# One transpose per tile of probabilities, and a router whose high and low weights share one stationary block

## The chip, the core and the metric

The kernel runs on one core of a Trainium2 chip. The core has TensorE (PE; its weight loads are a row of their own, PEld), VectorE (DVE), ScalarE (ACT), GpSimd (POOL) and SyncE (SP), which starts most of the transfers. The metric is the device time of one execution in microseconds, lower is better. Where a text speaks of the kernel before, its time is the median of three runs, 304.88 us (304.15 to 305.09).

## What is computed

One gated cross-attention block and one mixture-of-experts block, on 32 sequences of 64 tokens with 256 features. Cut to what matters:

```python
# x: (32, 64, 256), ctx: (32, 64, 256)
h = layernorm(x)
q, k_new, v_new = h @ wq.T, h @ wk.T, h @ wv.T
k = concat([ctx, k_new], axis=1)          # 128 keys per sequence: 64 of ctx, 64 new
v = concat([ctx, v_new], axis=1)
attn = softmax(q @ k.T / 16)              # no mask is applied
x = x + tanh(g_xattn) * (attn @ v) @ wo.T

h = layernorm(x)
probs = softmax(h @ gate_w.T)             # 8 experts, the two best of a token are kept
y = sum over the two of probs[e] * expert_e(h)       # silu(h @ fc1.T) * (h @ fc2.T) @ proj.T
y = y + sigmoid(h @ shared_gate_w.T) * shared(h)     # the same form, 704 wide
x = x + tanh(g_ffn) * y
```

All is float32. The kernel does its large products in split form: a value is kept as a high part, rounded to the type fp32r, and a low part, value minus high part, and a product is the sum of three matmuls, high by high, high by low and low by high (`THREE`).

## The kernel before, in words

The 2048 tokens are four chunks of 512 (`c`), each four tiles of 128 tokens (`j`). A tile holds two sequences (64 tokens each). The program is written out by hand for each engine, and the order in which each does its work is the order of the code; semaphores tie the engines together. It has these stages, in microseconds of the profiled execution: start (0 to 27), attention (27 to about 116), shared expert for three chunks together with loading of the expert weights (116 to 200), the 39 tiles of the routed experts (200 to 274), and the rest with the final sums.

In the attention stage a tile of scores is one bank of 128 rows (queries of both sequences) by 256 columns: the first half are new keys of both sequences, the second half keys of the context of both. A query needs the columns of its own sequence alone, so of each row two blocks of 64 are used. The work of one tile:

- `scores` (PE), six matmuls of 256 columns; `row_max` (VectorE), two reductions, one for each half of the partitions; `exps` (ScalarE), two exponentials, which write the used blocks into a buffer `PR` (one of two). The unused blocks of `PR` were set to zero at the start (L1233).
- `probs_t` (PE, L498): two transposes of 128x128, one for the new keys and one for the context.
- `probs_hi` (ScalarE) copies the 128x256 result to the high part `PT[0]`; `probs_lo` (VectorE) subtracts it to give the low part `PT[1]`. In the profile both stand under the helper's line and the names `ew_hi` and `ew_lo`, since the buffers are views of one large tensor (`EW`) that later holds the expert weights: L769 ACT `ew_hi<-bank` 128x256 and L1002 DVE `ew_lo<-bank,ew_hi` 128x256, 16 each, are these and nothing else.
- `values` (PE), twelve matmuls, then `v_hi` (ScalarE) and `v_lo` (VectorE), 128x512.
- `attend` (PE), six matmuls. The first waits for `probs_hi`, the second for `v_lo`, the third for `probs_lo`. `residual` (VectorE) adds the input and takes statistics.

Between these stand `project` for the next chunk, whose results `project_hi` (ScalarE) and `project_lo` (VectorE) split, and, for the chunk before, `second_norm`, `router` and `logits`. `router(c)` (PE) is six matmuls with 72 columns of weights as the stationary side (9 are used) and 512 tokens moving, three for each half of the features. Its output of 9 rows is copied by ScalarE, transposed by four small PE transposes (L539), and copied by VectorE (L1089) for the softmax of the router (L1117 on). ScalarE's `route_exp` is a part of that softmax. GpSimd makes the low parts of the context keys (L1468), the reciprocal roots of the norms, and issues the scatters; its first work waits for the constants.

In the code printed below, `own_keys` picks the columns of one sequence out of a bank, and `ring(base, j)` gives the count that frees one of two buffers.

## Time and profile before

| what | value |
|---|---|
| median of 3 runs | 304.88 us (304.15 to 305.09) |
| the profiled execution | 305.98 us, span 304.2 us |
| mean granted TensorE clock | 0.986 |
| PE busy | 276.9 us, 91% of the span, 1785 matmuls |
| DVE busy | 215.7 us, 71%, 698 instructions |
| ACT busy | 170.6 us, 56%, 399 instructions |
| POOL busy | 131.1 us, 43%, 163 instructions |
| DMA | 40.18 MB, mean 132 GB/s |

The span goes from the first to the last instruction; the execution's own time has 1.8 us more around it. Busy time is no critical path: an engine may be busy with work that nobody waits for. A matmul's duration in the rows overlaps the next one's, so what a matmul costs is read from the distance between starts, not from its length. The same holds, less strongly, for VectorE and ScalarE.

### The profile page before, as it was taken

Reading aid. Unit: us, or ns where it says so; the run is one execution under the profiler, and the core shown is the slowest. Engines: PE = TensorE matmul, PEld = TensorE weight load, DVE = VectorE, ACT = ScalarE, POOL = GpSimd, SP = SyncE. Lnnn points to the kernel's source line nnn. Section 1 sums busy time; section 2 is a strip of 40 time slices with the busy share of each in tenths; the row PEclk is TensorE's granted clock in tenths of the full one; section 3 lists DMA queues with packets and bytes.
Section 4 is the critical chain, followed back from the end, with each engine's and each line's share of the span. In section 5 each row is a group of like instructions: output and inputs, shape, how many; then the busy total and the mean of one; then the engine's idle time right before and its main releaser. Section 6 shows DMA issues by size and latency. Waiting matters only on the chain.

```text
span 304.2 us, 5865 instructions
## 1 busy us (share of the span) xinstructions
PE 276.9 (91%) x1785; PEld 249.0 (82%) x1785; DVE 215.7 (71%) x698; ACT 170.6 (56%) x399; POOL 131.1 (43%) x163
## 2 busy tenths in 40 slices
PE   0978989999999789799999999799999999999992
PEld 1867968888788667489888888689999999998891
DVE  2664777879968948766776775877787777863285
ACT  1565676777756546555325455456667666664230
POOL 1350361361587154732333000037777777786000
PEclk9997999999999999999999999999999999999996
DMA  6451107203028031433233665258888888866796
GB/s 196 173 176 69 70 11 239 82 21 122 1 77 280 1 110 53 151 130 120 92 123 128 188 232 185 59 134 139 136 136 138 137 137 143 126 71 69 239 353 239
DMA packets 30510, 40.18 MB, mean 132 GB/s; under 512 B 2960, under 2 KB 26640, under 8 KB 30480
## 3 DMA queue, kind: packets, MB, share of 16 engines
q1 hardware_dynamic: 22336, 29.53, 31.0%
q0 software_dynamic: 7152, 9.57, 19.0%
q10 hardware_dynamic: 992, 0.71, 0.9%
q8 instruction: 15, 0.25, 0.3%
q14 instruction: 15, 0.12, 0.1%
HBM read 22.68 MB, written 17.11 MB: 131 GB/s over the span
## 4 chain that ended last, share of the span: by engine, by line
PE 55%; DVE 23%; ACT 8%; issue 6%; POOL 3%; DMA 3%; DVEq 0%; ACTq 0%; SPq 0%; POOLq 0%
PE bank L415 43%; PE bank L654 6%; DVE ew_lo L1002 4%; ACT ew_hi L769 3%; PE bank L747 3%; DVE work L1332 3%; PE bank L703 3%; DVE xt_lo L1002 2%; ACT sh_hi L769 2%; DMA consts_sb<-consts_dram 2%; DVE work L1354 2%; DVE neg_max L1046 2%; ACT work L801 1%; DVE sh_lo L1002 1%; DMA weight_stage<-ew_dram 1%
## 5 line engine op out<-in xcount | busy, mean ns | idle before, releaser
L1522 POOL DMA_INDIRECT y_d<-work,dest_of_slot x39 | 60.5, 1552 | 56.3 <-DVE dest_of_slot L1378 54.7
L415 PE MATMUL bank<-ew_hi,xt_hi 128*128 (+2 forms) x172 | 53.8, 322 | 1.1 <-DVE xt_lo L1002 0.8
L415 PE MATMUL bank<-ew_lo,xt_hi 128*128 (+2 forms) x172 | 51.9, 302 | 0.0
L415 PE MATMUL bank<-ew_hi,xt_lo 128*128 (+1 forms) x133 | 40.5, 305 | 0.0
L1002 DVE TENSOR_TENSOR xt_lo<-bank,xt_hi 128x256 fp32r<-128x256 f32 (+2 forms) x90 | 35.7, 398 | 3.0 <-ACT xt_hi L769 1.5
L1482 POOL DMA_INDIRECT xs_d<-xn_all,slot_of_pair x32 | 32.0, 1001 | 10.1 <-issue 7.3
L415 PE MATMUL bank<-ew_hi 128*128 128x256 f32 (+1 forms) x100 | 31.5, 321 | 3.9 <-DVE ew_lo L1002 2.0
L1002 DVE TENSOR_TENSOR ew_lo<-bank,ew_hi 128x512 fp32r<-128x512 f32 (+1 forms) x41 | 22.7, 581 | 16.9 <-ACT ew_hi L769 16.8
L769 ACT ACTIVATE xt_hi<-bank 128x256 fp32r<-128x256 f32 (+1 forms) x90 | 32.7, 409 | 3.5 <-PE bank L747 2.2
L415 PE MATMUL bank<-xt_hi,sw_hi 128*128 128x512 f32 x88 | 34.6, 394 | 0.0
L415 PE MATMUL bank<-xt_lo,sw_hi 128*128 128x512 f32 x88 | 34.5, 392 | 0.0
L415 PE MATMUL bank<-xt_hi,sw_lo 128*128 128x512 f32 x88 | 34.4, 390 | 0.0
L415 PEld LDWEIGHTS bank<-ew_hi,xt_hi 128*128 128x128 f32 (+1 forms) x172 | 32.5, 189 | 1.7 <-DVE xt_lo L1002 1.0
L415 PEld LDWEIGHTS bank<-ew_lo,xt_hi 128*128 128x128 f32 (+1 forms) x172 | 32.7, 190 | 0.1
L415 PE MATMUL bank<-ew_hi,ew_lo 128*128 128x256 f32 (+1 forms) x100 | 31.1, 318 | 1.5 <-DVE ew_lo L1002 1.5
L415 PE MATMUL bank<-ew_lo,ew_hi 128*128 128x256 f32 (+1 forms) x100 | 30.8, 315 | 1.7 <-DVE ew_lo L1002 1.1
L769 ACT ACTIVATE sh_hi<-work 128x512 fp32r<-128x512 f32 (+1 forms) x24 | 15.2, 632 | 25.5 <-DVE work L1332 24.2
L654 PE MATMUL bank<-sw_hi,sh_hi 128*128 128x256 f32 x96 | 27.4, 290 | 2.0 <-DVE sh_hi L1002 1.9
L769 ACT ACTIVATE ew_hi<-bank 128x512 fp32r<-128x512 f32 (+1 forms) x45 | 21.7, 517 | 10.7 <-PE bank L415 6.9
L654 PE MATMUL bank<-sw_lo,sh_hi 128*128 128x256 f32 x96 | 27.0, 286 | 0.0
L930 ACT ACTIVATE work<-bank 128x512 f32<-128x512 f32 (+1 forms) x24 | 14.3, 594 | 21.9 <-PE bank L415 21.9
L415 PEld LDWEIGHTS bank<-ew_hi 128*128 128x128 f32 x100 | 19.5, 196 | 7.0 <-ACT ew_hi L769 3.7
(159 smaller groups left out, 688.5 us busy)
## 6 DMA issues: line engine op xcount, KB each, us to landing
work<-xs_d SPq DMA_DIRECT2D x39, 136.0 KB, 2.5
weight_stage<-ew_dram SPq DMA_DIRECT2D x10, 486.5 KB, 3.7
ew_hi<-y_d SPq DMA_DIRECT2D x8, 512.0 KB, 7.4
y_d<-work SPq DMA_DIRECT2D x6, 512.0 KB, 3.9
work<-ctx_t_dram SPq DMA_DIRECT2D x4, 512.0 KB, 3.5
xn_all<-x_dram SPq DMA_DIRECT2D x3, 512.0 KB, 6.5
xs_d<-pad_row SPq DMA_DIRECT2D x9, 136.0 KB, 1.8
weight_stage<-sw_dram SPq DMA_DIRECT2D x3, 384.0 KB, 3.2
```

Source lines behind the costliest of these rows:

```text
L415: last = nc.tensor.matmul(dst, a, b, start=(n == 0), stop=(n == len(pairs) - 1))
L654: last = nc.tensor.matmul(B[4 + t][:, 0:D], h[:, t * P:(t + 1) * P], w, start=(j == 0 and n == 0), stop=(j == S_FULL and n == len(parts) - 1))
L703: last = nc.tensor.transpose(rows_bank(n)[:, k * P:(k + 1) * P], EX[:, w, k * P:(k + 1) * P], ident)
L747: last = nc.tensor.transpose(B[4 + v][:, i * P:(i + 1) * P], EH[:, v, i * P:(i + 1) * P], ident)
L769: return nc.scalar.activation(dst, src, ACT.Copy, scale=scale)
L930: nc.scalar.activation(STH[0:rows, j % 2, :], B[pair(s, j)][0:rows, :], ACT.Silu).then_inc(a_th, 1)
L1002: return nc.vector.tensor_tensor(dst, src, hi.bitcast(F32), ALU.subtract)
L1046: last = nc.vector.tensor_reduce(nmx[r, j % 2:j % 2 + 1], own_keys(B[4 + j % 2], b), mybir.AxisListType.XY, ALU.max, negate=True)
L1332: nc.vector.tensor_tensor(SHF[0:rows, j % 2, :], STH[0:rows, j % 2, :], h2, ALU.mult).then_inc(v_h, 1)
L1354: nc.vector.tensor_scalar(SX2[:, t, :], B[4 + t][:, 0:D], GS[:, T:T + 1], None, ALU.mult).then_inc(v_z, 1)
L1482: nc.gpsimd.indirect_dma_start(out=xs_d, out_offset=bass.IndirectOffsetOnAxis(ap=POS[:, i, n:n + 1], axis=0), in_=XN[:, n, :], in_offset=N ...
L1522: nc.gpsimd.indirect_dma_start(out=y2_d, out_offset=bass.IndirectOffsetOnAxis(ap=IX[:, n:n + 1], axis=0), in_=EY[:, n % 4, :], in_offset=None,
```

## The change

The score columns get another order: new keys of sequence 0 (64), context keys of both (128, with the two sequences swapped), new keys of sequence 1 (64). The exponentials of a query now go into one dense block of 128 columns (`PR` is half as wide and needs no zeros). One transpose turns this block. In the result, the four quarters of 64x64 belong to two different sequences and two different kinds of key; `probs_hi` and `probs_lo` put each quarter where it belongs in `PT`, two quarters with one instruction on partitions 0 to 63 and two with one on 64 to 127. The other four quarters of `PT` must be zero: GpSimd clears them once, at the start, in place of VectorE's clearing of `PR`. The helper `own_probs` gives the destination; `own_half` does the same for the new keys, whose blocks are now apart.

In the router, the 72 stationary columns hold the high parts in columns 0 to 8 and the low parts in columns 32 to 40. A matmul with the high part of the tokens gives both products at once. So four matmuls do for six; the product of low weights and low tokens comes along and is added too. ScalarE copies 41 rows for 9, the transposes have 41 columns for 9, and VectorE adds the two parts where it copied.

The names in the profile change with it: line numbers move by a few (L415 is L419, L498 is L501, L1002 is L1007).

```diff
+RW_LO = 32
+RW_ROWS = RW_LO + N_E + 1
-NEW, OLD = 0, 1
+OLD = slice(SEQ, 3 * SEQ)
...
-        RW = [sb(f"router_{s}", [P, KD, RW_COLS], F32R) for s in ("hi", "lo")]
+        RW = sb("router", [P, KD, RW_COLS], F32R)
-        KC = [[e.rearrange("p (m j x n) -> p m j x n", m=KD, j=TPC, x=2) for e in half]
+        KC = [[e.rearrange("p (m j n) -> p m j n", m=KD, j=TPC) for e in half]
-        PT = [e[:, 8704:9216].rearrange("p (r x n) -> p r x n", r=2, x=2) for e in EW]
+        PT = [e[:, 8704:9216].rearrange("p (r x s n) -> p r x s n", r=2, s=2, x=2) for e in EW]
...
-        LGT = WK[0:N_E + 1, 4096:4608]
-        PR = WK[:, 4608:5120].rearrange("p (r x s n) -> p r x s n", r=2, x=2, s=2)
+        LGT = WK[0:RW_ROWS, 4096:4608]
+        PR = WK[:, 4608:4864].rearrange("p (r x n) -> p r x n", r=2, x=2)
+        ZERO = WK[:, 4864:5120]
...
             def scores(c, j):
-                             [(q[a][:, m, j * P:(j + 1) * P], keys[b][:, m, j, :, :].rearrange("p x n -> p (x n)"))
+                             [(q[a][:, m, j * P:(j + 1) * P], keys[b][:, m, j, :])
...
             def probs_t(c, j):
-                for x in range(2):
-                    last = nc.tensor.transpose(B[j % 2][:, x * P:(x + 1) * P],
-                                               PR[:, j % 2, x, :, :].rearrange("p s n -> p (s n)"), ident)
-                last.then_inc(p_pt, 1)
+                nc.tensor.transpose(B[j % 2][:, 0:P], PR[:, j % 2, :, :].rearrange("p x n -> p (x n)"), ident).then_inc(p_pt, 1)
...
             def attend(c, j):
-                             [(PT[a][:, j % 2, x, :], VO[b][:, j, x, :]) for x in range(2) for a, b in THREE], waits)
+                             [(PT[a][:, j % 2, x, :, :].rearrange("p s n -> p (s n)"), VO[b][:, j, x, :]) for x in range(2) for a, b in THREE], waits)
...
             def router(c):
-                             [(RW[a][:, k, :], XT[b][:, c, k, :]) for k in range(KD) for a, b in THREE], waits)
+                             [(RW[:, k, :], XT[b][:, c, k, :]) for k in range(KD) for b in range(2)], waits)
...
             def logits(c):
-                    last = nc.tensor.transpose(B[7][:, j * 16:j * 16 + N_E + 1], LGT[:, j * P:(j + 1) * P],
-                                               ident[0:N_E + 1, 0:N_E + 1])
+                    last = nc.tensor.transpose(B[7][:, j * 2 * RW_LO:j * 2 * RW_LO + RW_ROWS], LGT[:, j * P:(j + 1) * P],
+                                               ident[0:RW_ROWS, 0:RW_ROWS])
...
             def project_hi(c, i):
-                    copy(KC[c % 2][0][:, i - 2, :, NEW, :], bank[:].rearrange("p (j n) -> p j n", j=TPC)).then_inc(a_qk, 1)
+                    copy(own_half(KC[c % 2][0], i - 2), bank[:].rearrange("p (j s n) -> p j s n", j=TPC, s=2)).then_inc(a_qk, 1)
...
             def exps(c, j):
-                    last = nc.scalar.activation(PR[r, j % 2, :, b, :], own_keys(B[4 + j % 2], b),
+                    last = nc.scalar.activation(PR[r, j % 2, :, :], own_keys(B[4 + j % 2], b),
...
             def probs_hi(c, j):
-                copy(PT[0][:, j % 2, :, :], B[j % 2][:, 0:2 * P].rearrange("p (x n) -> p x n", x=2)).then_inc(a_pt, 1)
+                if (c, j) == (0, 0):
+                    act.wait_ge(pt_zero, 2)
+                for b in range(2):
+                    last = copy(own_probs(PT[0], j, b), B[j % 2][b * SEQ:(b + 1) * SEQ, 0:P].rearrange("p (s n) -> p s n", s=2))
+                last.then_inc(a_pt, 1)
...
-                copy(LGT, B[6][0:N_E + 1, :]).then_inc(a_lg, 1)
+                copy(LGT, B[6][0:RW_ROWS, :]).then_inc(a_lg, 1)
...
-                    sub(keys[1][:, i - 2, :, NEW, :], bank[:].rearrange("p (j n) -> p j n", j=TPC),
-                        keys[0][:, i - 2, :, NEW, :]).then_inc(v_qk, 1)
+                    sub(own_half(keys[1], i - 2), bank[:].rearrange("p (j s n) -> p j s n", j=TPC, s=2),
+                        own_half(keys[0], i - 2)).then_inc(v_qk, 1)
...
             def probs_lo(c, j):
-                sub(PT[1][:, j % 2, :, :], B[j % 2][:, 0:2 * P].rearrange("p (x n) -> p x n", x=2),
-                    PT[0][:, j % 2, :, :]).then_inc(v_pt, 1)
+                for b in range(2):
+                    last = sub(own_probs(PT[1], j, b), B[j % 2][b * SEQ:(b + 1) * SEQ, 0:P].rearrange("p (s n) -> p s n", s=2),
+                               own_probs(PT[0], j, b))
+                last.then_inc(v_pt, 1)
...
-                nc.vector.tensor_copy(LG[:, c * TPC:(c + 1) * TPC, :],
-                                      B[7][:, 0:TPC * 16].rearrange("p (j n) -> p j n", j=TPC)[:, :, 0:N_E + 1]).then_inc(v_lg, 1)
+                both = B[7][:, 0:TPC * 2 * RW_LO].rearrange("p (j x n) -> p j n x", j=TPC, x=2)[:, :, 0:N_E + 1, :]
+                nc.vector.reduce_sum(LG[:, c * TPC:(c + 1) * TPC, :], both, AX_X).then_inc(v_lg, 1)
...
-            nc.vector.memset(WK[:, 4608:5120], 0.0)
...
-                sub(RW[1][:], RWF[:], RW[0][:]).then_inc(rw_lo, 1)
+                low = slice(RW_LO, RW_ROWS)
+                sub(RW[:, :, low], RWF[:, :, low], RW[:, :, 0:N_E + 1]).then_inc(rw_lo, 1)
...
-                        last = nc.gpsimd.tensor_tensor(keys[1][:, k, j:j + 2, OLD, :],
+                        last = nc.gpsimd.tensor_tensor(keys[1][:, k, j:j + 2, OLD],
-                                                       keys[0][:, k, j:j + 2, OLD, :].bitcast(F32), ALU.subtract)
+                                                       keys[0][:, k, j:j + 2, OLD].bitcast(F32), ALU.subtract)
+            nc.gpsimd.memset(ZERO, 0.0).then_inc(pt_zero, 1)
+            pool.wait_ge(pt_zero, 1)
+            for half in EW:
+                for at in (8704, 8960):
+                    last = nc.gpsimd.tensor_tensor(half[:, at:at + 256], ZERO, ZERO, ALU.subtract)
+            last.then_inc(pt_zero, 1)
...
+def own_half(keys, m):
+    return keys[:, m, :, :].rearrange("p j (y n) -> p j y n", n=SEQ)[:, :, 0:4:3, :]
+def own_probs(probs, j, b):
+    rows = probs[b * SEQ:(b + 1) * SEQ, j % 2, :, :, :].rearrange("p x s n -> p (x s) n")
+    return rows[:, 2:0:-1, :] if b else rows[:, 0:4:3, :]
...
-    ctx = a["ctx_2048"].reshape(N_TOK, D)
+    ctx = a["ctx_2048"].reshape(N_T, 2, SEQ, D)[:, ::-1].reshape(N_TOK, D)
...
-    rw[:, :, :N_E + 1] = rows(np.concatenate([a["L0_ffn_gate_w"], a["L0_ffn_shared_gate_w"]], 0))
+    rw[:, :, :N_E + 1] = rw[:, :, RW_LO:RW_ROWS] = rows(np.concatenate([a["L0_ffn_gate_w"], a["L0_ffn_shared_gate_w"]], 0))
```

On VectorE the change shows at every tile. Here the end of the expert selection of chunk 0 and tile (2,0): `v_lo`, `probs_lo`, then the selection's next part. Before:

```order
L1130 MAX_INDEX work<-work 128x8 x4
L1133 CAST work<-work 128x8
L1002 TENSOR_TENSOR ew_lo<-bank,ew_hi 128x512
L1002 TENSOR_TENSOR ew_lo<-bank,ew_hi 128x256
L1141 TENSOR_TENSOR work<-work 128x32 x2
L1143 TENSOR_TENSOR work<-work 128x8x4
L1144 SCALAR_TENSOR_TENSOR work<-work 128x40
```

After:

```order
L1137 MAX_INDEX work<-work 128x8 x4
L1140 CAST work<-work 128x8
L1007 TENSOR_TENSOR ew_lo<-bank,ew_hi 128x512
L1007 TENSOR_TENSOR ew_lo<-bank,ew_hi 64x2x64 x2
L1148 TENSOR_TENSOR work<-work 128x32 x2
L1150 TENSOR_TENSOR work<-work 128x8x4
L1151 SCALAR_TENSOR_TENSOR work<-work 128x40
```

The one subtraction of 128x256 has become two of 64 partitions by 2x64, at the same place in the row; what stands before and behind is the same.

And a little later on VectorE, `v_lo`, `probs_lo` of (2,2) and the logits of chunk 1. Before:

```order
L1002 TENSOR_TENSOR ew_lo<-bank,ew_hi 128x512
L1002 TENSOR_TENSOR ew_lo<-bank,ew_hi 128x256
L1089 COPY logits<-bank 128x36
L1117 TENSOR_REDUCE work<-logits 128x4
L1118 TENSOR_TENSOR work<-logits,work 128x32
```

After:

```order
L1007 TENSOR_TENSOR ew_lo<-bank,ew_hi 128x512
L1007 TENSOR_TENSOR ew_lo<-bank,ew_hi 64x2x64 x2
L1097 TENSOR_REDUCE logits<-bank 128x36
L1124 TENSOR_REDUCE work<-logits 128x4
L1125 TENSOR_TENSOR work<-logits,work 128x32
```

The pair stands ahead of the sum that replaces the copy of the logits, so the softmax of the router is behind both.

On TensorE, the end of `attend(1, 1)`, `router(0)`, `values(1, 2)`, `probs_t(1, 2)`, `logits(0)` and the start of the projection. Before, from the last matmul of `attend` to the first of `values`:

```order
L415 MATMUL bank<-ew_hi,ew_lo 128x256
L415 MATMUL bank<-xt_hi,router_hi 72x512
L415 MATMUL bank<-xt_lo,router_hi 72x512
L415 MATMUL bank<-xt_hi,router_lo 72x512
L415 MATMUL bank<-xt_hi,router_hi 72x512
L415 MATMUL bank<-xt_lo,router_hi 72x512
L415 MATMUL bank<-xt_hi,router_lo 72x512
L415 MATMUL bank<-ew_hi,xt_hi 128x256
```

After:

```order
L419 MATMUL bank<-ew_hi,ew_lo 128x256
L419 MATMUL bank<-xt_hi,router 72x512
L419 MATMUL bank<-xt_lo,router 72x512
L419 MATMUL bank<-xt_hi,router 72x512
L419 MATMUL bank<-xt_lo,router 72x512
L419 MATMUL bank<-ew_hi,xt_hi 128x256
```

Two matmuls of 72x512 are gone, those with `router_lo`, and nothing has moved past anything else. The transposes behind `values(1, 2)`, with the last two matmuls of that and the first of `project(2, 2)`; the first piece is before, the second after:

```order
L415 MATMUL bank<-ew_lo,sw_hi 128x256
L415 MATMUL bank<-ew_hi,sw_lo 128x256
L498 MATMUL bank<-consts_sb,work 128x128 x2
L539 MATMUL bank<-consts_sb,work 128x9 x4
L415 MATMUL bank<-ew_hi 128x512
```

```order
L419 MATMUL bank<-ew_lo,sw_hi 128x256
L419 MATMUL bank<-ew_hi,sw_lo 128x256
L501 MATMUL bank<-consts_sb,work 128x128
L540 MATMUL bank<-consts_sb,work 128x41 x4
L419 MATMUL bank<-ew_hi 128x512
```

One transpose for two, and four small ones with 41 columns for 9.

## Rows read from the trace of the kernel before

**Rows 1.** The page's chain of waits, share of the span by engine.

```profile
PE 55%; DVE 23%; ACT 8%; issue 6%; POOL 3%; DMA 3%; DVEq 0%; ACTq 0%; SPq 0%; POOLq 0%
```

**Rows 2.** Busy time by stage: window, length, busy us (instructions), clock, DMA.

```profile
14.00:27.00 13.00, 10.96 (x62) 9.93 (x61) 7.66 (x20) 8.13 (x21) 5.25 (x8) 0.87 0.43 143
27.00:120.00 93.00, 85.40 (x565) 73.69 (x564) 71.82 (x247) 61.13 (x151) 41.75 (x81) 1.00 0.26 86
```

**Rows 3.** The chain in order of time: start us, us, engine, work, line.

```profile
21.91 4.64 PE bank L415 x24
...
28.87 0.41 PE bank L498 x2
...
51.74 0.87 ACT ew_hi L769 x2
...
58.94 0.34 DVE ew_lo L1002
...
59.33 3.56 PE bank L415 x22
62.88 0.22 PE bank L498 x2
...
127.43 1.62 PE bank L415 x6
...
130.12 3.07 PE bank L654 x24
```

**Rows 4.** Groups by shape: names, count | busy us, mean ns | idle before.

```profile
L1002 DVE TENSOR_TENSOR ew_lo<-bank,ew_hi 128x256 fp32r<-128x256 f32 x16 | 6.7, 416 | 0.4 <-ACT ew_hi L769 0.4
L498 PE MATMUL bank<-consts_sb,work 128*128 128x128 f32 x32 | 6.2, 275 | 2.0 <-DVE xt_lo L1002 1.5 <-ACT work L830 0.5
L769 ACT ACTIVATE ew_hi<-bank 128x256 fp32r<-128x256 f32 x16 | 6.1, 379 | 0.8 <-PE bank L498 0.8
...
L539 PE MATMUL bank<-consts_sb,work 9*128 9x9 f32 x16 | 1.6, 208 | 0.7 <-ACT work L769 0.7
...
L1117 DVE TENSOR_REDUCE work<-logits 128x4 f32<-128x32 f32 x4 | 0.7, 187 | 0.1
...
L1002 DVE TENSOR_TENSOR router_lo<-router_f,router_hi 128x144 fp32r<-128x144 f32 x1 | 0.3, 304 | 0.0
```

**Rows 5.** VectorE's timeline in the expert stage: start us, us, then as above.

```profile
230.86 0.28 DVE L1002 TENSOR_TENSOR xt_lo<-bank,xt_hi 128x128 fp32r<-128x128 f32 x1
231.15 0.29 DVE L1002 TENSOR_TENSOR xt_hi<-bank,xt_hi 48x128 fp32r<-48x128 f32 x1
231.48 0.42 DVE L1002 TENSOR_TENSOR xt_lo<-bank,xt_hi 128x256 fp32r<-128x256 f32 x1
231.82 0.14 DVE L1377 COPY weight_of_slot<-work 128x1 f32<-128x1 f32 x1
```

**Rows 6.** VectorE's timeline at the start of chunk 1, `first_lo` and `row_max`.

```profile
48.37 0.68 DVE L1002 TENSOR_TENSOR ew_lo<-bank,ew_hi 128x512 fp32r<-128x512 f32 x1
48.97 0.58 DVE L1046 TENSOR_REDUCE neg_max<-bank 64x1 f32<-64x128 f32 x2
```

**Rows 7.** VectorE's timeline, three instructions that had to wait: [idle before <-releaser].

```profile
21.16 1.29 DVE L1002 TENSOR_TENSOR ew_lo<-bank,ew_hi 128x512 fp32r<-128x512 f32 x2 [1.86 <-ACT ew_hi L769]
...
63.55 1.02 DVE L1002 TENSOR_TENSOR ew_lo<-bank,ew_hi 128x512 fp32r<-128x512 f32 x2 [0.22 <-ACT ew_hi L769]
...
93.64 0.69 DVE L1002 TENSOR_TENSOR sw_lo<-bank,sw_hi 128x512 fp32r<-128x512 f32 x1 [0.56 <-ACT sw_hi L769]
```

**Rows 8.** TensorE's timeline within `router(0)`.

```profile
60.13 0.40 PE L415 MATMUL bank<-xt_lo,router_hi 128*72 128x512 f32 x1
60.36 0.39 PE L415 MATMUL bank<-xt_hi,router_lo 128*72 128x512 f32 x1
```

**Rows 9.** GpSimd's timeline in the start.

```profile
6.88 0.19 POOL L1438 TENSOR_TENSOR ln_bias<-ln_mean_var,consts_sb 128x2 f32<-128x2 f32 x1 [6.44 <-DMA consts_sb<-consts_dram]
...
14.12 3.28 POOL L1468 TENSOR_TENSOR ew_lo<-work,ew_hi 128x256 fp32r<-128x256 f32 x4 [4.48 <-ACT ew_hi L769]
```

7 lines of the change are left out of this document (4 added, 3 removed).

## The prediction, made before the changed kernel ran

> **What bounds the kernel now.** I read the views in this order: the chain of waits by engine, the busy time by stage, the chain in order of time through the attention stage, then the timelines of VectorE and TensorE there, then the groups of instructions by shape. The reader is to see four things.
>
> First, the chain is PE for 55% and VectorE for 23% of the span [rows 1], and in the four chunks of the attention stage (27 to 120 us) TensorE is busy for 85.40 of 93 us, VectorE for 71.82 [rows 2]. Second, the two alternate on the path there: a TensorE stretch of 22 matmuls (3.56 us), in which four of `attend`, the six of `router` and the twelve of `values` stand, is preceded by a VectorE piece `ew_lo` of 0.34 us, which is `probs_lo` [rows 3]. So what sets TensorE going again is the very instruction that the change splits. Third, all that is edited lies before about 130 us; from `pj(0, 0)` on, code and sizes are the same, the chain is relative to earlier work, and a gain or loss before it is carried to the end one for one. Fourth, where the router's savings land, VectorE has little idle time left behind them: 0.22 us in chunk 1 and 0.56 us in chunk 2 [rows 7].
>
> Call the tiles (chunk, tile), 16 in all.
>
> **What is taken away.**
> - One of two probability transposes per tile. Two take 0.22 us of the chain at 62.88 [rows 3], so one is 0.11 us of TensorE. The first, at 28.87, runs at the lower clock, 0.41 us for two with overlapping ends [rows 3]; I take 0.17. Only where TensorE itself is the path does it count: (0,0) and (0,1), together 0.28. Elsewhere TensorE then waits for ScalarE or VectorE, or, in (2,2) and (2,3), for the VectorE work reckoned below.
> - Two of six router matmuls per chunk, 0.23 us apart (60.13 to 60.36) [rows 8], so 0.46 per chunk. Router 3 (the 1.62 us piece at 127.43) [rows 3] and router 2, in a stretch of the same make as that at 59.33, are on the path with nothing close behind: 0.46 each. Router 0 is released into `v_hi` and then `v_lo` of (1,2), before which VectorE is idle only 0.22 us [rows 7]: it counts for 0.22, and VectorE is late next. Router 1 comes below.
> - The low part of the router weights: 128x144 at 304 ns [rows 4] becomes 18 elements; 126 fewer at about 1 ns leaves 0.13 less, in the run of VectorE work at the end of chunk 0, which is on the path: 0.13.
> - VectorE's clearing of the probability buffer at the start: VectorE is idle 1.86 us later on before it is waited for [rows 7], so it is worth nothing.
>
> **What is added.**
> - `probs_hi` and `probs_lo` become two instructions on 64 partitions, 128 elements each, where one did 128x256. For VectorE the nearest rows are a 128x128 subtraction and one of 48x128 that begins at partition 64, in the expert stage. They start at 230.86 and 231.15, and the next, from partition 0 again, at 231.48; this next one is a 128x256, and its successor starts 0.34 us after it [rows 5]. So a 128x256 gives way after 0.34 us, though it lasts 0.42, while an instruction before or after a change of partitions gives way only when it has ended. A pair of halves occupies 0.29 + 0.33 = 0.62, which is 0.28 more than now (O), and its end comes at 0.29 + 0.29 = 0.58 after the start, 0.17 after the 416 ns [rows 4] of now (L). The pair of `row_max` halves shows the same, 0.58 us for two [rows 6].
> - O counts where the next VectorE instruction is the path, L where TensorE waits for the pair. By what the chain shows behind each tile: L at (0,3), (1,3), (3,1), (3,2), (3,3), 5 x 0.17 = 0.85. O at (1,2), where the softmax of router 0 follows and ScalarE waits for it, at (2,0) and (3,0), where the expert selection of an earlier chunk follows, and at (1,1), where VectorE runs on without a gap: 4 x 0.28 = 1.12. (0,0) to (0,2) and (1,0) have idle time behind them.
> - Chunk 2 from (2,1) on: TensorE gains 0.46 by router 1 and 0.22 by two transposes, less L. But VectorE's path through (2,2), the softmax and (2,3) gets 0.28 + 0.04 + 0.28 longer. From the new start of `values` it is 0.29 early (0.46 - 0.17), 0.03 late after (2,2), and the pair of (2,3) ends the idle 0.56 us before 93.64 [rows 7]: `project_lo(3,3)` comes 0.31 us earlier. That is all this chunk gives: 0.31.
> - ScalarE's pair: a 128x512 and a 128x256 take 0.87 us together, the latter 379 ns [rows 3, 4], so the former gives way after 0.49, somewhat under 1 ns an element. Two halves then cost little more than one; if each cost a full 128x256, it would be 0.38 more. On the path is one, at (1,0); the others lie beside `v_lo`. I take 0.05, nearest to the pace seen.
> - `logits`: the copy becomes a sum of 72 elements; a reduction of 32 takes 187 ns [rows 4], 40 more at 1 ns: 0.04, on the path once. Its transposes have 41 columns for 9: 208 ns against 275 for 128 columns [rows 4], so about 0.02 for one at most; 0.04 for the last four, on the path.
> - POOL clears four 128x256 blocks, beside a clearing of the source. Four such take 3.28 us [rows 9]; POOL has nothing before 6.88, having been idle for 6.44 [rows 9]. Hidden, with over 2 us to spare. If it were not, every microsecond past that would count in full.
>
> **Sum.** Gains 0.28 + 0.22 + 0.31 + 0.46 + 0.46 + 0.13 = 1.86. Losses 0.85 + 1.12 + 0.05 + 0.04 + 0.04 = 2.10. Net 0.24 us longer: the profiled execution, 305.98 us with a span of 304.2, would be 306.2. The median of the runs is 304.88, 1.1 below the profiled one; I apply the same difference, 305.1 us.
>
> **Two rules, weighed.** The hold seen at 231.15 is what the Trainium skill states (VectorE: DVE Perf Modes, section on two Vector instructions with no wait between them): an instruction whose input or output starts in another group of 32 partitions than the last starts only when all earlier ones have finished. By it every second half and every successor is held, in agreement with the row of 0.29 us. Against it stands the table of the same page (section on the TRN2 errata), 120 cycles plus one per element from PSUM at 0.96 GHz: an estimate from it is 0.26 us for a half and 0.39 for the whole, so 0.12 for either O or L, which leads to about 0.9 us shorter than before, near the first rival below. This trace has 0.42 for the whole and shows the hold, so I go by the rows.
>
> **The rivals.**
> - *The halves overlap.* If the second half and its successor start as early as unchanged neighbours do, a 128x512 gives way after 0.60 (48.37 to 48.97) [rows 6] and a 128x256 after 0.34, hence 128 elements after 0.21: the pair costs 0.42, and O = L = 0.08. The sum: gains 0.28 + 0.13 + 0.22 + 0.46 + 0.22 + 0.46 + 0.46 = 2.23, losses 10 x 0.08 + 0.13 = 0.93, net 1.30 shorter, 303.6 us. For it: halves on disjoint partitions have no conflict. Against it: both the 0.29 and the 0.58 for two.
> - *VectorE becomes the path throughout* (the slower side). Behind `probs_lo`, `residual` waits for TensorE and VectorE alike; from the point where VectorE's idle time ahead of it is under O - L = 0.11, the whole O counts. Then five tiles cost 0.11 more each (0.55), router 1 and 2 give nothing (0.31 + 0.46 lost): 0.24 + 1.32 = 1.56 longer, 306.4 us. For it: VectorE already is 23% of the chain and gets 16 x 0.28 = 4.5 us more occupied time. Against it: it is busy 71.82 of 93 us, and chunk 3 has gaps in it.
> - *The clock falls.* In the stretch of 14 to 27 us the granted clock is 0.87 on average and later full [rows 2]: TensorE fell to the lower of its two levels (1.2 for 2.4 GHz) in the scores of chunk 0, after a wait. These 24 matmuls took 4.64 us there, 24 of the same width take 3.07 at the full clock [rows 3], 1.57 more. Fewer matmuls give longer waits. One more such fall in the attention stage makes 0.24 + 1.57 = 1.81 longer, 306.7 us. Against it: with TensorE busy for over nine tenths of that stage, 3 us less work still leave it far busier than it was ahead of that fall.
>
> **How the numbers follow.** My forecast 0.50, overlap 0.24, VectorE throughout 0.17, the clock 0.04, the rest (hidden slack) 0.05. A measurement of this kernel tells 0.3%, 0.9 us, from no change. Overlap gives nearly all of faster (0.21), the forecast's own spread of some 0.6 us gives 0.05 on that side; most of the two slower cases (0.18) and 0.05 of the forecast give 0.23; the rest, 0.51, is no change. The range runs from the overlap case to that of VectorE throughout, 303.6 to 306.4, which leaves out 2 in 10. The likeliest case alone: 304.4 to 305.9.
>
> **What would show it.** In the profile after: `probs_lo` as 32 instructions of about 290 ns, the second 0.29 after the first and the successor 0.33 after the second; at 0.2, the overlap case holds. TensorE loses about 3.6 us of work, 16 transposes and 8 matmuls, and its idle time in 27 to 120 us grows by nearly as much. The chain's VectorE share rises, PE's falls. `router` stands as 16 matmuls. POOL's clearing ends before 5 us. The prediction is wrong in its core if the stage from 27 to 130 us becomes over 1 us shorter, or if ScalarE's halves show up on the path in more than one or two tiles.

## The result, and the profile after

The changed kernel takes 306.36 us (median of 20 runs, 304.56 to 308.6), the kernel before 304.59 us (20 runs beside them, 302.56 to 306.48). The ratio is 1.0058, interval 1.0039 to 1.0077: slower by about 1.8 us. The forecast was 305.1 us, no change; the time lies in the range, at the slow end of it, and on the side that had a chance of 0.23. A second measurement of the changed kernel, with other runs of before, gave 1.0037 (1.0011 to 1.0063). A ratio is not the quotient of the medians given with it, and executions over 1.5% above the fastest of their kernel are left out of it, two of the twelve of e3.

The profiled execution of the changed kernel is 305.6 us, span 303.8, mean granted clock 0.986; that of before was 305.98, 304.2, 0.986. The two profiled executions alone would say that nothing changed. What is inside them differs. The page's busy times and chain, after:

```profile
PE 274.9 (90%) x1761; PEld 245.7 (81%) x1761; DVE 218.8 (72%) x713; ACT 174.2 (57%) x415; POOL 135.0 (44%) x168
...
PE 49%; DVE 27%; ACT 9%; issue 8%; POOL 3%; DMA 2%; DVEq 0%; ACTq 0%; POOLq 0%; SPq 0%
```

TensorE lost 2.0 us of work and 6 points of the chain against [rows 1]; VectorE, ScalarE and "issue" took them. Busy time by stage, columns as in [rows 2]:

```profile
14.00:27.00 13.00, 8.94 (x59) 7.65 (x59) 7.95 (x16) 7.90 (x21) 3.02 (x5) 1.00 0.42 145
27.00:120.00 93.00, 83.57 (x536) 71.32 (x535) 72.95 (x258) 62.99 (x161) 42.19 (x81) 0.98 0.25 86
```

The clock was 0.87 at the start and 1.00 in the attention stage before; now it is 1.00 at the start and 0.98 in the attention stage. A stretch at the lower clock (from here on, a fall) stands in each of the two, at different places, and the start was quicker after: `scores(0,0)` begins at 19.56 us for 21.91. So the two spans, 0.4 us apart, say nothing of the change. The groups that answer to [rows 4]:

```profile
L1007 DVE TENSOR_TENSOR ew_lo<-bank,ew_hi 64x128 fp32r<-64x128 f32 x32 | 9.1, 284 | 0.7 <-ACT ew_hi L770 0.5
...
L770 ACT ACTIVATE ew_hi<-bank 64x128 fp32r<-64x128 f32 x32 | 8.5, 266 | 0.9 <-PE bank L501 0.7
...
L501 PE MATMUL bank<-consts_sb,work 128*128 128x128 f32 x16 | 4.4, 277 | 2.3 <-DVE xt_lo L1007 1.9 <-ACT work L831 0.4
...
L540 PE MATMUL bank<-consts_sb,work 41*128 41x41 f32 x16 | 1.8, 237 | 0.7 <-ACT work L770 0.7
...
L1097 DVE TENSOR_REDUCE logits<-bank 128x36 f32<-128x72 f32 x4 | 0.9, 233 | 1.9 <-PE bank L540 1.8
...
L1007 DVE TENSOR_TENSOR router<-router_f,router 128x18 fp32r<-128x18 f32 x1 | 0.2, 173 | 0.0
```

The halves last 284 ns on VectorE (290 were forecast) and 266 ns on ScalarE, where the whole 128x256 had 379. VectorE's timeline at tile (1,1):

```profile
55.11 0.68 DVE L1007 TENSOR_TENSOR xt_lo<-bank,xt_hi 128x512 fp32r<-128x512 f32 x1
55.71 0.58 DVE L1007 TENSOR_TENSOR ew_lo<-bank,ew_hi 64x128 fp32r<-64x128 f32 x2
56.32 0.69 DVE L1041 SCALAR_TENSOR_TENSOR ew_lo<-bank,ew_hi 128x512 fp32r<-128x512 f32 x1
```

The pair ends after 0.58 us and its successor starts 0.61 after it, against 0.62 forecast from [rows 5]. This is the rule of the Trainium skill that the prediction weighed (VectorE: DVE Perf Modes, section on two Vector instructions with no wait between them); the trace agrees with it.

**GpSimd** clears the quarters early and unseen:

```profile
0.73 0.31 POOL L1480 MEMSET work<- 128x256 f32 x1 [0.29 <-POOLq L1626]
1.12 1.18 POOL L1484 TENSOR_TENSOR ew_hi<-work 128x256 fp32r<-128x256 f32 x2
2.27 1.17 POOL L1484 TENSOR_TENSOR ew_lo<-work 128x256 fp32r<-128x256 f32 x2
4.80 0.20 POOL L1445 TENSOR_TENSOR ln_bias<-ln_mean_var,consts_sb 128x2 f32<-128x2 f32 x1 [1.36 <-DVE ln_mean_var L1022]
```

It is done at 3.44 us. Its next work starts 2.08 us earlier than in [rows 9], because the constants landed sooner in this execution. The repeated kernel before shows that too (its TensorE starts at 4.24 us, not 6.84), so it is no effect of the change.

**Where the clock fell.** TensorE's timeline at `attend(3, 1)` and `router(2)`, after:

```profile
102.65 0.35 PE L419 MATMUL bank<-ew_hi 128*128 128x256 f32 x1 [1.12 <-DVE work L1172]
103.15 0.39 PE L419 MATMUL bank<-ew_lo,ew_hi 128*128 128x256 f32 x1
104.25 0.58 PE L419 MATMUL bank<-ew_hi,ew_lo 128*128 128x256 f32 x1 [0.71 <-DVE ew_lo L1007]
104.63 0.42 PE L419 MATMUL bank<-ew_hi 128*128 128x256 f32 x1
104.84 0.41 PE L419 MATMUL bank<-ew_lo,ew_hi 128*128 128x256 f32 x1
105.05 0.41 PE L419 MATMUL bank<-ew_hi,ew_lo 128*128 128x256 f32 x1
105.27 0.63 PE L419 MATMUL bank<-xt_hi,router 128*72 128x512 f32 x1
105.69 0.63 PE L419 MATMUL bank<-xt_lo,router 128*72 128x512 f32 x1
```

and the same place before:

```profile
104.46 0.35 PE L415 MATMUL bank<-ew_hi 128*128 128x256 f32 x1 [0.73 <-DVE work L1165]
...
105.89 0.39 PE L415 MATMUL bank<-ew_hi,ew_lo 128*128 128x256 f32 x1 [0.55 <-DVE ew_lo L1002]
106.11 0.28 PE L415 MATMUL bank<-ew_hi 128*128 128x256 f32 x1
```

Two waits have grown from 0.73 and 0.55 us to 1.12 and 0.71. The first ends with VectorE's expert selection (L1172), which stands behind the pair of (3,0); the second ends with the pair of (3,1) itself. Behind them the matmuls of 256 columns start 0.21 us apart for 0.12, those of the router 0.42 for 0.23: the lower level of the clock, 1.2 GHz, for about 3 us. The granted clock of 104 to 112 us is 0.79 in this profile, and 1.00 in that of before.

**How the stage is read from here on.** The start of an execution varies by over 1 us (arrival of the constants, and the clock there). But the distance from the first `residual` to the later ones and to the first `pj` is the same within 0.03 us in the two profiles of the kernel before up to the first `pj`, though one had a fall at the start. So I use these distances. Up to the fall at (3,1) the two profiles of the changed kernel agree within 0.05 us, behind it within 0.16. In us, against the repeated kernel before:

| profile | (1,0) | (1,3) | (2,0) | (2,1) | (2,3) | (3,0) | (3,1) | (3,2) | (3,3) | pj(0,0) | pj to the end |
|---|---|---|---|---|---|---|---|---|---|---|---|
| before | 0.00 | 0.01 | 0.02 | 0.02 | 0.00 | 0.03 | 0.02 | 0.01 | 0.01 | 0.01 | -0.07 |
| after | 0.32 | 0.86 | 1.30 | 1.54 | 1.22 | 1.68 | 2.33 | 2.98 | 3.14 | 2.73 | 0.27 |
| after, waits filled (e4) | 0.29 | 0.85 | 1.28 | 1.51 | 1.18 | 1.63 | 1.79 | 1.48 | 1.64 | 1.22 | 0.44 |
| router alone (e1) | -0.12 | -0.45 | -0.46 | -0.45 | -0.88 | -0.85 | -0.86 | -1.34 | -1.34 | -1.77 | 0.19 |
| dense alone (e2) | 0.44 | 1.61 | 2.05 | 2.28 | 2.27 | 2.72 | 3.37 | 4.47 | 4.64 | 4.64 | -0.15 |
| dense alone, filled (e10) | 0.46 | 1.65 | 2.08 | 2.32 | 2.28 | 2.74 | 2.90 | 3.06 | 3.22 | 3.22 | -0.02 |
| ScalarE by columns (e6) | 0.05 | 0.47 | 0.91 | 1.14 | 0.67 | 1.13 | 1.77 | 2.51 | 2.66 | 2.23 | 0.34 |
| both by columns, filled (e9) | -0.04 | -0.17 | -0.10 | -0.02 | -0.66 | -0.50 | -0.44 | -0.85 | -0.79 | -1.20 | 0.22 |

Two of the rows behind this table are the first `residual` and that of (3,0) in the repeated kernel before, 68.98 us apart:

```profile
30.22 0.48 DVE L1069 SCALAR_TENSOR_TENSOR work<-bank,softmax_scale,xn_all 128x256 f32<-128x256 f32 x1
...
99.20 0.48 DVE L1069 SCALAR_TENSOR_TENSOR work<-bank,softmax_scale,xn_all 128x256 f32<-128x256 f32 x1
```

and after, 70.66 apart:

```profile
29.42 0.48 DVE L1076 SCALAR_TENSOR_TENSOR work<-bank,softmax_scale,xn_all 128x256 f32<-128x256 f32 x1
...
100.08 0.48 DVE L1076 SCALAR_TENSOR_TENSOR work<-bank,softmax_scale,xn_all 128x256 f32<-128x256 f32 x1
```

### The profile page after: what moved, and what is told of

The parts are those of the page before. It is cut to its first block, busy times and chain, and to the rows that moved or that the text cites. A ratio compares the mean times of both kernels' runs of the same rounds, so it can differ in the third digit from the quotient of the medians.

```text
span 303.8 us, 5853 instructions
## 1 busy us (share of the span) xinstructions
PE 274.9 (90%) x1761; PEld 245.7 (81%) x1761; DVE 218.8 (72%) x713; ACT 174.2 (57%) x415; POOL 135.0 (44%) x168
## 4 chain that ended last, share of the span: by engine, by line
PE 49%; DVE 27%; ACT 9%; issue 8%; POOL 3%; DMA 2%; DVEq 0%; ACTq 0%; POOLq 0%; SPq 0%
PE bank L419 37%; PE bank L655 6%; DVE ew_lo L1007 6%; ACT ew_hi L770 3%; PE bank L748 3%; DVE work L1339 3%; PE bank L704 3%; DVE neg_max L1051 2%; ACT sh_hi L770 2%; DVE xt_lo L1007 2%; DVE work L1361 2%; ACT work L802 1%; DVE work L1076 1%; DMA weight_stage<-ew_dram 1%; DVE sh_lo L1007 1%
## 5 line engine op out<-in xcount | busy, mean ns | idle before, releaser
L419 PE MATMUL bank<-ew_hi,xt_hi 128*128 (+2 forms) x172 | 54.0, 323 | 1.2 <-DVE xt_lo L1007 0.8
L419 PE MATMUL bank<-ew_lo,xt_hi 128*128 (+2 forms) x172 | 51.8, 301 | 0.0
L419 PE MATMUL bank<-ew_hi,xt_lo 128*128 (+1 forms) x133 | 40.6, 306 | 0.0
L1007 DVE TENSOR_TENSOR xt_lo<-bank,xt_hi 128x256 fp32r<-128x256 f32 (+2 forms) x90 | 35.7, 399 | 3.0 <-ACT xt_hi L770 1.5
L1495 POOL DMA_INDIRECT xs_d<-xn_all,slot_of_pair x32 | 32.8, 1025 | 10.1 <-issue 7.3
L419 PE MATMUL bank<-ew_hi 128*128 128x256 f32 (+1 forms) x100 | 30.9, 316 | 6.9 <-ACT ew_hi L770 3.1
L1007 DVE TENSOR_TENSOR ew_lo<-bank,ew_hi 64x128 fp32r<-64x128 f32 (+1 forms) x57 | 25.1, 460 | 15.2 <-ACT ew_hi L770 14.9
L419 PE MATMUL bank<-xt_hi,sw_hi 128*128 128x512 f32 x88 | 34.7, 394 | 0.0
L419 PE MATMUL bank<-xt_lo,sw_hi 128*128 128x512 f32 x88 | 34.5, 392 | 0.0
L419 PE MATMUL bank<-xt_hi,sw_lo 128*128 128x512 f32 x88 | 34.3, 390 | 0.0
L419 PEld LDWEIGHTS bank<-ew_hi,xt_hi 128*128 128x128 f32 (+1 forms) x172 | 32.6, 190 | 1.9 <-DVE xt_lo L1007 1.0
L419 PE MATMUL bank<-ew_hi,ew_lo 128*128 128x256 f32 (+1 forms) x100 | 30.9, 316 | 2.7 <-DVE ew_lo L1007 1.8
L419 PEld LDWEIGHTS bank<-ew_lo,xt_hi 128*128 128x128 f32 (+1 forms) x172 | 32.9, 191 | 0.2
L419 PE MATMUL bank<-ew_lo,ew_hi 128*128 128x256 f32 (+1 forms) x100 | 30.4, 311 | 1.4 <-DVE ew_lo L1007 1.1
L770 ACT ACTIVATE ew_hi<-bank 64x128 fp32r<-64x128 f32 (+1 forms) x61 | 24.2, 421 | 6.1 <-PE bank L419 4.3
L419 PEld LDWEIGHTS bank<-ew_hi 128*128 128x128 f32 x100 | 18.9, 190 | 10.5 <-ACT ew_hi L770 6.9
```

Of the source, the lines that this page charges most:

```text
L419: last = nc.tensor.matmul(dst, a, b, start=(n == 0), stop=(n == len(pairs) - 1))
L770: return nc.scalar.activation(dst, src, ACT.Copy, scale=scale)
L1007: return nc.vector.tensor_tensor(dst, src, hi.bitcast(F32), ALU.subtract)
L1495: nc.gpsimd.indirect_dma_start(out=xs_d, out_offset=bass.IndirectOffsetOnAxis(ap=POS[:, i, n:n + 1], axis=0), in_=XN[:, n, :], in_offset=N ...
```

## The experiments

**e0, the kernel before once more.** No edit.

> The kernel before, unchanged, as a measure of what five rounds can tell and for a second profile. Every theory: ratio 1.000 within its interval. The pair of theories differs in the clock: if TensorE's fall to the lower clock at 22 to 27 us is a fixed trait of this kernel, this profile shows it there again, with full clock from 27 to 120 us; if it is a matter of chance or of how the start falls out, it is missing or elsewhere, and the time differs by about 1.5 us with it.

Measured: 304.29 us, ratio 0.9992 (0.9964 to 1.002), span 301.6. It has no fall at the start, and serves as the base of the table above.

**e1, the router's part alone; e2, the dense part alone.** The edits are the two halves of the change's diff: `RW`, `RW_LO`, `router`, `LGT`, `logits` in the one, the rest in the other.

> Only the router half of the change: high and low weights in one block, 4 matmuls for 6 per chunk, the sum of the two parts. Theory A (the sum of the prediction): router 0 counts for 0.22, routers 1 to 3 for 0.46 each, the low weights for 0.13, the logits cost 0.08, so 1.65 us shorter, ratio 0.9946. Rival B (less TensorE work costs a further fall of the clock in chunk 3, as the profile of the changed kernel shows at 104 us): 1.65 shorter and about 1.5 longer, ratio 0.999 to 1.001, with a granted clock under 0.95 in the stage of 97 to 120 us.

> Only the other half: one transpose per tile, the split copies, the clearing by GpSimd; the router as before. Theory A (held pairs on the path): 0.28 gained, pairs cost 0.85 + 1.12 and in chunk 2 some 0.2, ScalarE 0.05, so about 1.9 us longer, ratio 1.006. Rival B (the clock does it): the same pairs and a fall of the clock in chunk 3, 3.4 us longer, ratio 1.011; and if the pairs were cheap and only the clock mattered, 1.0 to 1.5 us longer with the fall at 97 to 120 us.

Measured: the router alone 303.86 us, ratio 0.9962 (0.9932 to 0.9992); the dense part alone 308.57 us (6 runs), 1.0112 (1.0065 to 1.0159). So the change is one part that gains and one that loses two to three times as much. The sum of the two, 1.0074, is above the 1.0058 and 1.0037 of both together; its own uncertainty is some 0.006, so it contradicts neither. In the profiles the two add up: -1.77 and +4.64 at the first `pj` make 2.87, and the whole change has 2.73.

**e3, both splits by columns.** Left out is the placement of the quarters, so that all instructions start at partition 0.

```diff
-                for b in range(2):
-                    last = copy(own_probs(PT[0], j, b), B[j % 2][b * SEQ:(b + 1) * SEQ, 0:P].rearrange("p (s n) -> p s n", s=2))
+                for x in range(2):
+                    last = copy(PT[0][:, j % 2, x, :, :], B[j % 2][:, 0:P].rearrange("p (s n) -> p s n", s=2))
```

and the same in `probs_lo`.

> The changed kernel, but probs_hi and probs_lo are split by columns, two instructions of 128 partitions x 128 elements, in place of two on 64 partitions each. It leaves out the placing of the quarters, so the probabilities are not the reference's; all instruction counts and sizes per partition are as in the changed kernel. Theory A (the change of partitions holds the second half and its successor, 0.28 or 0.17 us a tile on the path): the pair takes 0.42 for 0.61, and the kernel is 1.5 us faster than the changed one, 1.3 us shorter than before, ratio 0.996. Rival C (two instructions cost what they cost, wherever they begin): the pair stays at about 0.6 and the ratio is that of the changed kernel, 1.006.

Measured: 304.73 us, 0.9959 (0.9922 to 0.9996); the median without the two slowest, as in the ratio, is 303.86. VectorE's timeline at tile (1,1) shows why:

```profile
57.57 0.48 DVE L1007 TENSOR_TENSOR ew_lo<-bank,ew_hi 128x128 fp32r<-128x128 f32 x2
57.96 0.68 DVE L1041 SCALAR_TENSOR_TENSOR ew_lo<-bank,ew_hi 128x512 fp32r<-128x512 f32 x1
```

Two instructions with as many elements per partition, 281 ns each, give way to the next after 0.39 us for 0.61. It is not the second instruction that costs, but the change of partitions. The profile of e3 has a fall at 26.5 us and another at 105 us, so its row in the distances would mislead; e9 stands in the table in its place. ScalarE shows the same. The last row of each is `probs_hi` with the `project_hi` behind it, first after, then by columns; the repeated kernel before has 0.88 there for two instructions:

```profile
54.85 1.17 ACT L770 ACTIVATE ew_hi<-bank 64x128 fp32r<-64x128 f32 x3
```

```profile
56.70 0.94 ACT L770 ACTIVATE ew_hi<-bank 128x128 fp32r<-128x128 f32 x3
```

With halves by partitions 0.29 more, with halves by columns 0.06.

**e4, the waits at attend(3,1) filled.** After, with dead transposes, that is, transposes of the identity into a free bank that nobody reads:

```diff
                 for n, (a, b) in enumerate(pairs):
+                    if n in idle:
+                        keep(idle[n])
...
-  for x in range(2) for a, b in THREE], waits)
+  for x in range(2) for a, b in THREE], waits,
+                             {0: 8, 2: 5} if (c, j) == (LAST, 1) else {})
```

> The changed kernel, with 13 dead transposes of the identity at attend(3,1): eight ahead of its first matmul and five ahead of its third, where TensorE waits. They leave nothing out and fill most of two waits, 1.12 and 0.71 us in the profile of the changed kernel, behind which the matmuls stand 0.21 us apart for 3 us instead of 0.12. Theory: these two waits, made longer by the change (0.73 and 0.55 before), let the granted clock fall. Then the stretch of 104 to 112 us shows a clock of 1.00 where it was 0.79, router(2) is 0.23 us a matmul again, the time from the first residual of chunk 3 to the first pj is 1.45 us shorter, and the runs come to about 305.0 us, ratio to before 1.001. Rival: the fall comes now and then by chance, whatever TensorE does in that wait; then it stays in this profile or is absent by chance, and the ratio stays at 1.006.

**e5, the changed kernel once more.** No edit.

> The changed kernel once more, unchanged. Two things are read from it: whether the clock falls at attend(3,1) in a second profile too, and the ratio on the chip and in the rounds of the other three kernels. Theory (the longer waits let it fall): clock 0.79 at 104 to 112 us again, the same waits of about 1.1 and 0.7 us ahead, ratio 1.005 to 1.007. Rival (falls there come by chance): no fall in this profile; the residuals of chunk 3 then stand 1.45 us earlier against the first one.

Measured: e4 305.71 us, 1.0011 (0.9986 to 1.0036); e5 306.03 us, 1.0037 (1.0011 to 1.0063). The means of their 12 runs each are 0.74 us apart, with an uncertainty of 0.67. In e5 the same waits and the same fall stand again; the stretch of 104 to 112 us there, then in e4:

```profile
104.00:112.00 8.00, 7.01 (x39) 5.76 (x40) 4.32 (x16) 2.76 (x9) 4.25 (x8) 0.80 0.29 104
```

```profile
104.00:112.00 8.00, 7.09 (x50) 5.73 (x48) 5.18 (x18) 2.81 (x10) 4.76 (x8) 1.00 0.30 104
```

TensorE in e4:

```profile
101.88 1.04 PE L575 MATMUL bank<-consts_sb 128*128 128x128 f32 x8
103.15 0.36 PE L421 MATMUL bank<-ew_hi 128*128 128x256 f32 x1 [0.24 <-DVE work L1180]
103.65 0.39 PE L421 MATMUL bank<-ew_lo,ew_hi 128*128 128x256 f32 x1
103.88 0.71 PE L575 MATMUL bank<-consts_sb 128*128 128x128 f32 x5
104.74 0.38 PE L421 MATMUL bank<-ew_hi,ew_lo 128*128 128x256 f32 x1 [0.16 <-DVE ew_lo L1015]
104.96 0.28 PE L421 MATMUL bank<-ew_hi 128*128 128x256 f32 x1
```

VectorE's work ends no earlier (the first matmul still waits for it), but the matmuls behind are 0.12 us apart again, and the first `pj` comes 1.5 us earlier than after. Filling the waits removes the fall and its 1.35 to 1.5 us in the profile: with the change of `probs_t` and unfilled waits there are five profiles (after, e2, e3, e5, e6), all with the fall, and with filled waits three (e4, e9, e10), all without it. The ratio is the 1.001 expected; the median is 0.7 us above the 305.0.

**e6, ScalarE alone by columns.** The edit of e3 in `probs_hi` only; VectorE keeps its halves by partitions.

> The changed kernel, with ScalarE's probs_hi as two instructions of 128x128, split by columns on all 128 partitions; VectorE's probs_lo stays split by partitions. Left out: the placement of the quarters in the high part. With both engines split by columns (the run before this) the time was 304.73 against 306.36 for the changed kernel, 2.4 us apart at equal mean clock. This run divides that between the two engines. Theory: both hold at a change of partitions, ScalarE too (v_hi and its pair took 1.17 us for 0.88 before, and 0.94 by columns), but the path is VectorE's in most tiles; ScalarE's share is what stands in the profile at (0,2), (0,3), (1,0), (2,0), (3,0), 0.5 to 0.7 us: 305.8 us, ratio 1.004. Rival: ScalarE's hold is the larger part, since what it delays, VectorE delays again: 304.9 or less, ratio under 1.001. Rival: nothing on ScalarE counts: 306.4, ratio 1.006.

Measured: 305.69 us, 1.0028 (1.0004 to 1.0051), the forecast of the first theory. In the table ScalarE's hold is worth 0.25 at (1,0) and 0.14 more up to (1,3), and 0.5 by (3,0); by the first `pj` 0.3 to 0.5 of it is left. Tile by tile against e5, it appears at (1,0), (1,2) and (2,2). The rest of the distance to e9 is VectorE's.

**e7, the router's part with the start filled.** 16 dead transposes ahead of `scores(0,0)` and 14 ahead of `probs_t(0,0)`.

> The kernel before with the router's part of the change alone, and 30 dead transposes of the identity at the start: 16 ahead of scores(0,0), 14 ahead of probs_t(0,0), where TensorE waits 2.2 and 1.9 us. Nothing is left out. The router's part alone measured 0.9962, 303.86 us. Theory: in some executions the clock falls after the first of these waits (1.57 us in the profile of before, at 23 to 27 us), so runs with the waits filled lose the upper part of their spread: median 303.2, ratio 0.994, clock 1.00 from 14 to 27 us. Rival: that fall is rare, the transposes cover nothing in the median, ratio 0.996. Rival, slower: the transposes outlast the waits (30 at 0.11 us are 3.3 of 4.1 us) or delay what follows by queueing, ratio 0.998 or more.

Measured: 302.76 us, 0.9937 (0.9904 to 0.9969). The clock is 1.00 from 14 to 27 us. The profile has a fall between 120 and 130 us instead (clock 0.83 there), where TensorE waits 0.74 and 0.68 us ahead of `router(3)` and `logits(3)`; e1 had nearly the same waits there (0.76 and 0.68), the same instructions around them, and no fall. So neither the waits nor the work beside them tell the two apart; what does is not shown.

**e8, a longer wait in the kernel before.**

```diff
-                step(nc.vector.tensor_scalar(PAY[:, :, t, 1].rearrange("p i t -> p t i"), V8[:, t, 0:TOP], TG[:, 1:2], None, ALU.mult))
+                for _ in range(3 if c == 1 else 1):
+                    step(nc.vector.tensor_scalar(PAY[:, :, t, 1].rearrange("p i t -> p t i"), V8[:, t, 0:TOP], TG[:, 1:2], None, ALU.mult))
```

> The kernel before, with one small VectorE instruction of the expert selection of chunk 1 (a product of 128x8, 0.23 us to the next) issued three times for once, ahead of attend(3,1). Nothing is left out. TensorE's first wait at attend(3,1) so grows from 0.73 to about 1.19 us, the second stays near 0.55. Theory: it is the length of these waits that lets the clock fall (with 0.73 and 0.55 it never fell in four profiles, with 0.89 and 0.61 or more it fell in all five), so it falls here too, in the kernel before: clock about 0.8 at 104 to 112 us, and 0.46 + 1.35 = 1.8 us longer than before, 306.4 us, ratio 1.006. Rival: the fall comes from something else of the change (the dense transposition, the halves); then only the 0.46 us is seen, 305.1 us, ratio 1.0015, clock 1.00.

Measured: 306.7 us, 1.004 (1.0003 to 1.0077). TensorE's timeline:

```profile
103.61 0.36 PE L415 MATMUL bank<-ew_hi 128*128 128x256 f32 x1 [1.27 <-DVE work L1166]
104.11 0.38 PE L415 MATMUL bank<-ew_lo,ew_hi 128*128 128x256 f32 x1
105.04 0.39 PE L415 MATMUL bank<-ew_hi,ew_lo 128*128 128x256 f32 x1 [0.55 <-DVE ew_lo L1002]
105.26 0.28 PE L415 MATMUL bank<-ew_hi 128*128 128x256 f32 x1
```

The first wait is longer than after (1.27 for 1.12), the two together are as long (1.82 for 1.83), and the clock does not fall: 0.54 us is all that the first `pj` is late. My theory that the first wait, or the two together, decide by their length is refuted by this profile. The profiles with a fall there (after, e2, e3, e5, e6) all have a second wait of 0.61 us or more, and one transpose less ahead of it; whether either matters, or the moment at which the waits come, was not tried, and what decides stays open. The runs do not decide it: 1.004 lies between the 1.0015 of the rival and the 1.006 of the theory, and 7 of 12 of this kernel have a mean clock under 0.985 and 16 of 34 of before beside them, no clear difference.

**e9, both by columns with the waits filled; e10, the dense part with the waits filled.** The edits of e3 and e2, each with that of e4 (seven and four transposes in e9).

> The changed kernel, with both splits by columns on all 128 partitions (the placement of the quarters is left out) and eleven dead transposes in the waits at attend(3,1), seven and four. It is what the change would be without the cost of the partition change and without the fall. Theory (costs add): the profile's distance from the first residual to the first pj is 0.74 - 1.35 = 0.6 us under that of before, the runs 0.9959 - 0.0044 = 0.9915, 302.0 us. Rival: the columns version's gain was chance of its runs (its profile showed 0.74 longer at the first pj), and with the fall filled it comes to 0.995, 303.1 us. Rival: the dead transposes push attend(3,1) back, no better than 0.996.

> The dense part of the change alone (router as before), with 13 dead transposes in the waits at attend(3,1). Nothing is left out. Theory (the fall is a fixed trait of the dense part and costs 1.35 us): no fall at 104 to 112 us, first pj 4.64 - 1.4 = 3.2 us later than before against the first residual, runs at 1.0112 - 0.0045 = 1.0067, 306.7 us. Rival: the dense part's excess over the whole change (its first pj 1.9 us later than that of the whole change) has another fall or wait in it that this does not touch: 307.5 us or more.

Measured: e9 303.31 us, 0.9926 (0.9896 to 0.9956); e10 307.84 us, 1.0078 (1.0042 to 1.0114). Both show the clock at 1.00 from 27 us to 200 us. (In e9 and e10, as in before, the fall at the start remains.) e10's first `pj` is at +3.22, as forecast; its ratio is 0.0011 above the forecast, within its interval. e9's is at -1.20, twice the forecast, since the profile of e3, from which that came, had a further fall at 26.5 to 29.9 us. Its runs, at 303.31 us, are nearer to the rival's 303.1 than to the 302.0 of the theory, the ratio nearer to the theory's 0.9915.

**e11, the router's part with all longer waits filled**: the 30 of e7, five and four at `attend(3,1)`, six ahead of `router(3)`, five ahead of `logits(3)`. `router(3)` and `logits` take their waits in another order, so that the transposes stand in them.

> The router's part alone, with dead transposes in all of TensorE's longer waits ahead of the expert stage: 16 and 14 at the start (as measured already, 302.76 us), five and four at attend(3,1), six ahead of router(3), five ahead of logits(3). Nothing is left out. Theory: every fall ahead of 200 us is preceded by such a wait (in the last profile of this kind there was one at 124 to 127 us, behind waits of 0.74 and 0.68), so none is left: clock 1.00 in every window up to 200 us, 302.3 us, ratio 0.992. Rival: the falls there are rare and the transposes cost what they save: 302.8, ratio 0.994. Rival, slower: keeping TensorE's queue full delays the router, which is on the path: 303.5 or more, 0.9965.

Measured: 302.15 us, 0.991 (0.9877 to 0.9942): 3 us faster than the kernel before beside it (305.21), and the fastest kernel of this study. About half of the 3 us is the clock, by the table below. Its stretches up to 200 us:

```profile
14.00:27.00 13.00, 11.74 (x88) 10.46 (x87) 8.26 (x19) 7.86 (x21) 3.96 (x6) 1.00 0.43 145
27.00:120.00 93.00, 86.70 (x579) 75.19 (x579) 72.42 (x250) 62.28 (x152) 44.82 (x84) 1.00 0.26 89
120.00:200.00 80.00, 77.34 (x465) 67.81 (x464) 58.56 (x145) 38.36 (x65) 20.66 (x22) 1.00 0.44 143
```

Its runs lie closer together, 301.69 to 303.75, where before has 303.12 to 306.94.

**Runs at equal clock.** Each run lists its mean granted clock, and within a kernel the time follows it: a line fitted through all runs, with each kernel's own mean taken out, has 0.196 us for 0.001 of clock, and 0.59 us of spread remain. Runs come in groups near 0.996, 0.991, 0.987 and 0.981, and one fall, about 3 us at half the clock in some 302, lowers the mean by 0.005 to 0.006, which is 1.0 to 1.2 us on the line. But the mean is no count of falls. The end of each profile stands at the lower level too, the last 5.2 us in e0 (from 296.4) and the last 2.2 in e8; e0 so has 0.991 without a fall before its end, and e8 0.991 with one, though from the first `pj` to the end the two differ by 0.03 us only. The line is therefore an average, and what follows is an estimate. Read off it at a clock of 0.991:

| kernel | mean clock | us at 0.991 | minus before |
|---|---|---|---|
| before (29, 35 and 34 runs) | 0.9869, 0.9865, 0.9863 | 303.98, 304.10, 304.21 | |
| after (20 and 12 runs) | 0.9858, 0.9859 | 305.39, 305.25 | +1.2 |
| before once more (e0) | 0.9892 | 304.04 | +0.1 |
| after, waits filled (e4) | 0.9891 | 305.13 | +1.0 |
| ScalarE by columns (e6) | 0.9851 | 304.73 | +0.6 |
| both by columns (e3) | 0.9853 | 303.09 | -0.9 |
| both by columns, filled (e9) | 0.9880 | 302.61 | -1.6 |
| router alone (e1) | 0.9849 | 302.46 | -1.5 |
| router, start filled (e7) | 0.9887 | 302.58 | -1.5 |
| dense alone (e2) | 0.9860 | 307.38 | +3.4 |
| dense alone, filled (e10) | 0.9897 | 307.27 | +3.1 |
| router, all filled (e11) | 0.9931 | 302.77 | -1.4 |
| before, longer wait (e8) | 0.9844 | 305.01 | +0.8 |

The last column's uncertainty is about 0.4 (0.5 for e2), from the spread of 0.59. As far as the line holds, it is the cost of a kernel's own order of work; the clock comes on top.

## Why the prediction was right and where it failed

The forecast was no change, with faster and slower about equally likely. The mechanism of the likeliest case stands: the change of partitions costs on VectorE, at the pair and its successor, what the expert stage's rows said. But the sum was +0.24, and at equal clock the change costs +1.2. That puts it where the rival "VectorE throughout" stood (+1.56), and the bound of 0.9 us for "no change" is passed. That the measured 306.36 us is within the range is owed to the width of the range, whose end, 306.4, is 0.04 us away, and not to the sum.

**Steps that held**, against the table and the rows. A pair occupies 0.61 (0.62 forecast), ends 0.17 late: L is seen at (3,1) (+0.16) and (3,3) (+0.16), O at (1,1) (+0.30). The transpose at (0,1) gives 0.11. The router low part 0.13: -0.12 at (1,0) in e1. Router 2 and 3: 0.48 and 0.43 at (3,2) and pj(0,0) in e1; router 0 gave 0.33 there, for 0.22. GpSimd's clearing is hidden. TensorE's busy time fell by 2.0 us only, where 3.6 was forecast, and in 27 to 120 us by 1.8 (85.40 to 83.57); that was not followed up, since recorded matmuls overlap and both profiles hold a slow stretch.

**The sum that failed** is the losses; up to the first `pj` and without the fall, it was to be +0.41 (without the 0.17 at (0,0), which lies ahead of the first `residual`), and e4 has +1.22. The terms, in the prediction's order:

- The transposition at (0,0), 0.17: from the transpose to the first `residual` it is 4.02 us in the repeated kernel before (26.20 to 30.22) and 4.02 in e5 (25.43 to 29.45). Nothing was gained there, nor with columns (4.01 in e9). The prediction also read the row at 28.87 as one at the lower clock; the granted clock from 26.3 to 29.3 us is 1.00, and e0 has the same 0.41 us.
- "On the path is one, at (1,0) ... I take 0.05" for ScalarE's pair. It is 0.25 (e6 against after). The step took two halves at the pace of one long instruction; but ScalarE's halves do not overlap either, 0.27 and 0.27, so the whole of 0.29 counts and not 0.05. e6 is 0.34 to 0.5 faster than after by the table, 0.5 at equal clock. The prediction named it as a sign that its core is wrong if this shows up in more than one or two tiles. It does, at three, (1,0), (1,2) and (2,2): ScalarE was part of the path, which the prediction left to VectorE and TensorE.
- O at (2,0) and (3,0), 0.28 each: 0.43 and 0.45 from the `residual` before to these. O counted the hold of the pair's direct successor alone, but there is a second one. From the `residual` of (1,3) to the row of `v_lo` and the pair of (2,0) e0 and e5 both take 5.50 us, so nothing is carried over from L at (1,3). The pair then costs its 0.28 (the next instruction starts 0.94 us behind the start of that row in e0 and 1.22 in e5). Four instructions on SBUF follow, and behind them the first that reads a bank again. In e0, then in e5:

```profile
74.68 0.24 DVE L1144 TENSOR_TENSOR_SCAN work<-work 128x40 f32<-128x40 f32 x1
74.84 0.66 DVE L1036 SCALAR_TENSOR_TENSOR sh_lo<-bank,sh_hi 128x512 fp32r<-128x512 f32 x1
```

```profile
75.05 0.24 DVE L1151 TENSOR_TENSOR_SCAN work<-work 128x40 f32<-128x40 f32 x1
75.33 0.69 DVE L1041 SCALAR_TENSOR_TENSOR sh_lo<-bank,sh_hi 128x512 fp32r<-128x512 f32 x1
```

  It starts 0.16 us behind the scan in e0 and only at its end, 0.28, in e5. At (2,0) it is 0.27 or 0.28 in all six profiles with VectorE's halves by partitions (after, e2, e4, e5, e6, e10) and 0.15 or 0.16 in before, e0, e1 and e8 and with columns (e3, e9). At (3,0) it is the same but for e3 and e9, which have 0.19 and 0.20. So the pair costs 0.28 and later 0.12.
- Chunk 2 from (2,1) on, 0.31 gained: 0.10 is (1.28 to 1.18). The pair of (2,1) costs 0.23 there; I had let it count only as 0.17 for TensorE, hidden by router 1. ScalarE's share of (2,2) stands here too. And the working itself slipped: a VectorE that is 0.03 and then 0.28 late ends an idle time of 0.56 only 0.25 early, not 0.31.
- (0,2) and (0,3): 0.23 in all, from -0.11 at (0,1) to +0.12, where idle time was to cover (0,2) and L to cost 0.17 at (0,3).
- Behind the first `pj` the kernels with the router's part are 0.15 to 0.44 us later (e7, with its fall there, 1.83). In e1 about half of it appears only after 266 us. It was not located.

Without the first and the last these make about 0.8 us up to the first `pj`, all of the distance from +0.41 to +1.22. e9 against e4 gives the whole price of the change of partitions, 2.4 us, of which 0.3 to 0.5 is ScalarE's; the prediction had 2.0 for all the pairs.

**The clock rival**, given 0.04. In the profiles of the changed kernel it happened as described: one fall in the attention stage, 1.35 to 1.5 us (1.57 forecast), and the time of that rival, 306.7, is nearer to the 306.36 than my own. The argument against it, that TensorE is busy for nine tenths of the stage, failed: an average over 93 us says nothing about the 2 us around one tile. But by the mean clock it is not the main reason why the kernel is slower. By the mean clock the runs of before lose as much to the lower level: it is 0.9863 to 0.9869 for them, 0.9858 for after. Neither of the two profiles of before has the fall at `attend(3,1)`, and one of them has a fall at the start; for the runs the places are not known. The difference of 0.001 is 0.2 us of the 1.8 (1.3 in e5); the order of the work is 1.2, and the remainder is within the uncertainty. Filling the waits took 0.74 us off the mean of the runs, with an uncertainty of 0.67, so the share of this fall in the runs is known no better than that. I should have forecast falls as a property of each execution, in both kernels, rather than as an event that a change adds.

**The halves-overlap rival**, 0.24: e3 and e9 are that case made real, with a pair of 0.39 for the 0.42 reckoned. The 0.9959 of e3 and the -1.20 of e9 at the first `pj` agree with the -1.30 that the rival was given; the 0.9926 of e9 is 2.3 us, more than that, with the waits at `attend(3,1)` filled as well. Its arithmetic was about right, its condition was not met.

## What to carry to other kernels

In this kernel, splitting one instruction into two cost little where both start at the same partition (0.05 us), and about a whole duration of a half (0.27 to 0.29 us) where they do not, on ScalarE as on VectorE; on VectorE a later instruction was held as well. Saving half of the transposes of the probabilities did not pay for 32 such splits, since VectorE and ScalarE release TensorE there. Where a gain on one engine leaves TensorE waiting, look at the granted clock around that wait and not at its mean over the stage, and try filling such waits with dead transposes: from e1 to e11 that was worth 0.005 of the time, about as much as the router's saved matmuls. Compare kernels by distances between marked instructions inside the profile, or, as an estimate, by runs at equal clock, before believing a difference of one microsecond between two spans.

## What the runs showed of the hardware that was not expected

- Two executions of one program agree within 0.03 us over 97 us of four engines' work, although one came to its first `residual` 2.7 us later; of the spread of some 1.0 us between runs of a kernel, 0.59 remains once the mean clock is taken out.
- The clock fell behind waits of 2.0 us and more at `scores(0,0)` in six of nine profiles (before, e2, e6, e8, e9, e10; not in after, e1, e5), never in the two where the wait was filled (e7, e11), nor there in the three where the wait came out at 1.1 to 1.5 us (e0, e3, e4); e3 has its fall later, at 26.5 us, behind a wait of 1.86 at `probs_t(0,0)`, which e0, e4 and three others (after, e1, e5) had, within 0.03 us, without one. It fell at `attend(3,1)` in five of five profiles with waits of 0.89 and 0.61 us or more that were not filled, but not in e8 with 1.27 and 0.55; and of e1 and e7, alike in work and waits at `router(3)`, only e7 has one there. A fall costs 1.1 us at the start (`scores(0,0)` to `probs_t(0,0)` takes 6.96 us with it and 5.82 without) and about 1.4 at `attend(3,1)`.
- ScalarE's 64x128 halves take 0.27 us each one after the other; the 128x128 halves give way after some 0.17.
- Behind two VectorE instructions of which the second starts at partition 64, not only the next instruction waits for the end of all before it, but once more the first that reads a bank again, five instructions later (0.28 us behind the scan for 0.16).
